# A mixture-of-experts and attention kernel on one core: slot table read first, no adds ahead of the first tile, tokens taken ahead of the gather

## What is computed

```
x = x + 0.5 * ffn(layernorm(x))
x = x + attn(layernorm(x))
x = x + 0.5 * ffn(layernorm(x))

ffn:  logits = x @ Wr;  two best of E = 8 experts per token, weights by softmax over the two
      pos = rank of the token within its expert;  kept = pos < cap  (cap = 2560)
      h = silu(xe @ W1[e]) * (xe @ W3[e])      (1024 wide)
      out[token] += weight * (h @ W2[e])
attn: KV = cumsum(K outer V);  Y = Q . KV per head (16 heads of 16);  a 16x16 map per head;  Y @ Wc.T
```

## Time and profile before

| | us |
|---|---|
| median of 3 runs | 3054.07 (3050.84 to 3055.57) |
| the profiled execution | 3048.99 |
| its span | 3047.3 |
| PE busy | 2854.6 (94%) |
| DVE, ACT, POOL busy | 1602.6, 1253.7, 1158.8 |
| mean granted clock of PE | 0.971 |

### The profile page before, as it was taken

The page is one execution under the profiler, slowest core; times in us unless marked ns, Lnnn a source line. Parts: engine busy times, 40 slices in busy tenths (PEclk is TensorE's granted clock), DMA queues, the critical chain, the costliest instruction groups (busy, mean ns, idle before and its releaser), DMA issues. The chain is left out here.

```text
span 3047.3 us, 54514 instructions
## 1 busy us (share of the span) xinstructions
PE 2854.6 (94%) x18727; PEld 2543.1 (83%) x18727; DVE 1602.6 (53%) x3791; ACT 1253.7 (41%) x2685; POOL 1158.8 (38%) x1560
## 2 busy tenths in 40 slices
PE   5379999999999999979999994999999999999997
PEld 3368898989899988868888884898998998898986
DVE  8843544454454545347778775345545454445443
ACT  5233434344444434334444442344434343444433
POOL 3654444444443434310111123443434443444432
PEclk9689999999999999989999996999999999999999
DMA  7542323232323312220111013323323232323221
GB/s 251 177 119 39 80 36 77 42 77 42 77 44 75 84 30 41 36 54 29 58 56 59 30 44 95 85 40 76 77 43 77 42 81 32 80 42 77 41 36 26
DMA packets 156550, 198.51 MB, mean 65 GB/s; under 512 B 15696, under 2 KB 128464, under 8 KB 156368
## 3 DMA queue, kind: packets, MB, share of 16 engines
q0 software_dynamic: 64128, 88.42, 17.6%
q1 hardware_dynamic: 81952, 97.30, 9.8%
q10 hardware_dynamic: 10288, 10.38, 1.0%
HBM read 124.32 MB, written 80.11 MB: 67 GB/s over the span
## 5 line engine op out<-in xcount | busy, mean ns | idle before, releaser
L1259 DVE TENSOR_TENSOR e_h_lo<-e_hid,e_h_hi 128x384 fp32r<-128x384 f32 (+1 forms) x640 | 383.7, 600 | 399.2 <-ACT e_h_hi L1219 399.2
L1256 DVE TENSOR_TENSOR e_hid<-e_ps,e_gate 128x384 f32<-128x384 f32 (+1 forms) x640 | 382.0, 597 | 308.4 <-ACT e_gate L1215 308.3
L1219 ACT ACTIVATE e_h_hi<-e_hid 128x384 fp32r<-128x384 f32 (+1 forms) x640 | 356.7, 557 | 444.1 <-DVE e_hid L1256 443.8
L1215 ACT ACTIVATE e_gate<-e_ps 128x384 f32<-128x384 f32 (+1 forms) x640 | 333.5, 521 | 330.7 <-PE e_ps L101 330.5
L99 PE MATMUL e_ps<-e_xT_hi,c_wa 128*128 128x384 f32 (+1 forms) x1280 | 454.5, 355 | 9.0 <-DVE e_yrow L1269 6.0
L99 PE MATMUL e_ps<-e_xT_hi,e_wb 128*128 128x384 f32 (+1 forms) x1280 | 460.3, 360 | 0.0
L100 PE MATMUL e_ps<-e_xT_lo,e_wb 128*128 128x384 f32 (+1 forms) x1280 | 455.1, 356 | 0.0
L101 PE MATMUL e_ps<-e_xT_hi,e_wb 128*128 128x384 f32 (+1 forms) x1280 | 455.0, 355 | 0.0
L101 PE MATMUL e_ps<-e_xT_hi,c_wa 128*128 128x384 f32 (+1 forms) x1280 | 449.7, 351 | 0.0
L100 PE MATMUL e_ps<-e_xT_lo,c_wa 128*128 128x384 f32 (+1 forms) x1280 | 449.7, 351 | 0.0
L433 POOL DMA_INDIRECT c_xrow<-normed_rows,e_token x320 | 347.8, 1087 | 156.6 <-issue 91.3
(11 more groups left out here) (297 smaller groups left out, 5189.5 us busy)
## 6 DMA issues: line engine op xcount, KB each, us to landing
c_raw<-w SPq DMA_DIRECT2D x204, 256.0 KB, 5.5
normed_rows<-r_xn SPq DMA_DIRECT2D x8, 1056.0 KB, 7.2
normed_rows<-mi_xn SPq DMA_DIRECT2D x8, 1056.0 KB, 4.7
x<-x ACTq DMA_DIRECT2D x8, 1024.0 KB, 12.3
out<-mi_x SPq DMA_DIRECT2D x8, 1024.0 KB, 5.3
r_xin<-x SPq DMA_DIRECT2D x7, 1024.0 KB, 11.0
c_raw<-x SPq DMA_DIRECT2D x7, 1024.0 KB, 8.1
c_xrow<-normed_rows,e_token POOLq DMA_INDIRECT x320
```

Of the source, the lines that this page charges most:

```text
L1215: act.activation(gate[:, f % 2, 0:n], ps1[f % 2][:, 0:n], ACT.Silu).then_inc(gated, 1)
L1219: act.activation(h[0][:, f, 0:n], hid[:, f % 2, 0:n], ACT.Copy).then_inc(h_high, 1)
L1256: dve.tensor_tensor(hid[:, f % 2, 0:n], ps3[f % 2][:, 0:n], gate[:, f % 2, 0:n], ALU.mult).then_inc(hid_ready, 1)
L1259: dve.tensor_tensor(h[1][:, f, 0:n], hid[:, f % 2, 0:n], h[0][:, f, 0:n].bitcast(F32), ALU.subtract).then_inc(h_ready, 1)
```

## The change

It has five parts.

1. `tiles` is split: `read_counts` keeps the one operation that reads PE's bank, where `tiles` stood; the other operations follow `read_table`, in the route phase behind the six `low_w` too, which themselves now follow `read_table`.
2. The first turn of an expert phase takes three blocks in place of four, waits for three gathers, and `high_x` and `low_x` behind it are 384 columns wide.
3. The single add of zeros and tile 0's four are gone; tile 1's four stay.
4. `meta(g + 1)` is done within tile g, behind its adds and ahead of its gather. `meta(0)` is done once ahead of the first tile, and the first expert is written out ahead of the loop over the other seven.
5. The loads of groups 1 and 2 of the middle phase's input are issued at the start of the middle phase.

```diff
+    def read_counts(self, dve):
+        dve.wait_ge(self.count_made, 1)
+        dve.tensor_scalar(self.lg[:, 0, :], self.rank_bank[:, self.RANK_AT:self.RANK_AT + E], float(CAP), float(P - 1),
+                          ALU.min, ALU.add).then_inc(self.count_read, 1)
...
     def tiles(self, dve, table):
...
-        dve.wait_ge(self.count_made, 1)
-        dve.tensor_scalar(units, self.rank_bank[:, self.RANK_AT:self.RANK_AT + E], float(CAP), float(P - 1), ALU.min,
-                          ALU.add).then_inc(self.count_read, 1)
...
     def load_x1(self, sp, x1, x1_g):
         for i in range(MG // 2):
             sp.dma_start(x1[:, 0, 2 * i:2 * i + 2], x1_g[0][:, 2 * i:2 * i + 2]).then_inc(self.x_first[i], 16)
-        for g in (1, 2):
-            sp.dma_start(x1[:, g], x1_g[g]).then_inc(self.x_loaded[g], 16)
...
-                r.tiles(dve, tiles_out)
+                r.read_counts(dve)
+                dve.wait_ge(r.tabled, T // P // QUAD)
+                r.read_table(dve, r.table_bank[:, 0:SCOLS], slot_token)
                 for q in range(LOW_BY_POOL, PIECES):
                     low_w(q)
-                dve.wait_ge(r.tabled, T // P // QUAD)
-                r.read_table(dve, r.table_bank[:, 0:SCOLS], slot_token)
+                r.tiles(dve, tiles_out)
...
-                def meta(g):
-
-                    pool.wait_ge(y_added, WORDS * g + 16)
+                def meta(g, adds):
+
+                    if adds:
+                        pool.wait_ge(y_added, WORDS * g - WORDS)
                     wait_alone(pool, held, g + 1, k.passed)
...
-                def tile(e, subs, at, behind, g):
-                    meta(g)
+                def tile(e, subs, at, behind, g, adds=True):
                     hold(e, subs, at, g)
-                    wait_alone(pool, y_kept, g + 1, k.passed)
-                    add(BIG)
+                    if adds:
+                        wait_alone(pool, y_kept, g + 1, k.passed)
+                        add(BIG)
+                    meta(g + 1, adds)
                     gather(behind, g)
...
-                wait_alone(pool, held, 1, k.passed)
-                add(1)
-                with pool.Fori(0, E) as e:
+                meta(0, False)
+                expert(0, adds=False)
+                with pool.Fori(1, E) as e:
                     expert(e)
 
                 n = total(pool)
-                meta(n)
                 wait_alone(pool, y_kept, n + 1, k.passed)
                 add(BIG)
-                pool.wait_ge(y_added, WORDS * n + WORDS + 16)
+                pool.wait_ge(y_added, WORDS * n)
...
-                def turn(n_loaded):
+                def turn(n_loaded, subs=BIG):
                     pe.wait_ge(x_loaded, n_loaded)
                     for half in range(KD):
-                        for sub in range(BIG):
+                        for sub in range(subs):
...
-                turn(WORDS)
+                turn(16 * SMALL, SMALL)
...
-                high_x(KD + 1)
+                high_x(KD + 1, SMALL * P)
...
-                low_x(1)
+                low_x(1, SMALL * P)
...
+                load(1)
+                load(2)
                 for g in range(MGS):
                     sp.wait_ge(x2_ready, MG * (g + 1))
...
                     if n == NCH + COUNT:
-                        r.tiles(dve, tiles_out)
+                        r.read_counts(dve)
...
                 dve.drain()
                 r.read_table(dve, tab[:], slot_token)
+                r.tiles(dve, tiles_out)
```

More of the change, by code:

```diff
@@ L1082, in hold, with expert @@
                     pool.tensor_copy(next_token[:, 0:subs], slot_token[:, bass.ds(at, subs)]).then_inc(next_held, 1)
-                def tile(e, subs, at, behind, g):
-                    meta(g)
+                def tile(e, subs, at, behind, g, adds=True):
                     hold(e, subs, at, g)
-                    wait_alone(pool, y_kept, g + 1, k.passed)
-                    add(BIG)
+                    if adds:
+                        wait_alone(pool, y_kept, g + 1, k.passed)
+                        add(BIG)
+                    meta(g + 1, adds)
                     gather(behind, g)
-                def expert(e):
+                def expert(e, adds=True):
                     f, big, small = counts(pool, e)
                     at = e * UPE
-                    tile(e, SMALL, at, pool.snap(at + SMALL), f)
+                    tile(e, SMALL, at, at + SMALL if isinstance(e, int) else pool.snap(at + SMALL), f, adds)
                     with pool.Fori(0, big) as t:
@@ L1133, in _ @@
                 add(SMALL)
-                wait_alone(pool, y_added, WORDS * n + WORDS + 16 * SMALL + 16, k.passed)
+                wait_alone(pool, y_added, WORDS * n + 16 * SMALL, k.passed)
                 pool.nop().then_inc(all_added, 1)
@@ L1201, in high_w, with high_x @@
                     act.activation(piece(slots[1 - s][:, 0], q), piece(raw, q), ACT.Copy).then_inc(w_high, 1)
-                def high_x(n):
+                def high_x(n, width=WIDE):
                     for half in range(KD):
                         act.wait_ge(x_turned, n + half)
-                        act.activation(xT[0][:, half, :], psx[:, half, :], ACT.Copy).then_inc(x_high, 1)
+                        act.activation(xT[0][:, half, 0:width], psx[:, half, 0:width], ACT.Copy).then_inc(x_high, 1)
                 def tile(e, s, subs, first, at, g):
@@ L1243, in low_w, with low_x @@
                                       ALU.subtract).then_inc(w_low, 1)
-                def low_x(n):
+                def low_x(n, width=WIDE):
                     for half in range(KD):
                         dve.wait_ge(x_high, n + half)
-                        ins = dve.tensor_tensor(xT[1][:, half, :], psx[:, half, :], xT[0][:, half, :].bitcast(F32),
-                                                ALU.subtract)
+                        ins = dve.tensor_tensor(xT[1][:, half, 0:width], psx[:, half, 0:width],
+                                                xT[0][:, half, 0:width].bitcast(F32), ALU.subtract)
                     ins.then_inc(x_ready, 1)
```

## The result

| | before | after |
|---|---|---|
| median of 4 runs, us | 3054.82 (3050.84 to 3055.69) | 3019.20 (3017.54 to 3019.95) |
| profiled execution, its span | 3048.99, 3047.3 | 3019.95, 3018.2 |

The ratio is 0.9885, with an interval of 0.9868 to 0.9902; 3022.9 was forecast. In three later series the kernel before had medians of 3052.68, 3052.90 and 3054.98, and the changed kernel, run once more, 3020.71 (3018.94 to 3021.25).

The account below looks back on a forecast made before the run. TensorE bounds the expert phases without gaps; gains lie in stalls at their starts and between blocks. 5.6 + 3.4 + 1.0 + 9.2 + 6.0 + 6.0 = 31.2 us off 3054.07 gave 3022.9 us, range 3015 to 3034.

Parts of the forecast that it names:

- turn stalls: Expert phases' starts: PE's waits for tile 1's gather, 1.97 and 7.24 us, would go, 9.2 us.
- read-out stalls: Expert phases' starts: tile 1's second banks waiting for tile 0's results to be read out, 3.58 + 2.44 = 6.0 us, would go.
- the clock: Behind three of the four stalls PE's granted clock was 0.66 to 0.84; full speed would return 6.0 us, ends 4 and 6.
- The route phase's end: Slot table read ahead of counts and low parts: route block ends 5.6 us sooner, ends 3.6 and 5.9.
- so SP is late next: Route phase's end: SP, done at 155.5, rather than POOL's drain (152.4 to 155.4) would end the block; 155.7 taken.
- The counts of the middle phase: Middle phase's end: counts leave the chain ahead of the picks and the gather, gaining 3.4 us.
- the narrow turn: Tile 0 of each expert phase: first transpose to first matmul, 3.44 us, shortens by 0.5 us a phase, 1.0 us.
- Part 4 at nothing: Every tile: waiting for the adds' landing ahead of the gather, 3.0 to 7.1 us, hides under 9.3 us cover; cost 0.
- A: Rival at the route phase's end: VectorE's subtracts and counts hold the gather, 3026.6 us; chance 0.12.
- C: Rival: blocks end as before, POOL's drain not set by the gather's landing, 9.0 us fail, 3031.9 us; chance 0.04.
- D: Rival in all tiles: POOL becomes the bound through the landing wait ahead of the gather, 3060 us and over; chance 0.03.
- B: Rival in tile 1: the four adds of zeros that stay keep the read-out stall, 3030.6 us; chance 0.08.

Follow-up runs that it names:

- Experiment ten: Changed kernel with expert 1's weights loaded at the start of expert phase 1's block, not at the route phase's end: 3016.29 us.
- experiment nine: Changed kernel plus six 128x512 VectorE subtracts with unused output behind the middle phase's table read, beside a gather without weight loads: 3020.69 us.
- experiment one: Changed kernel with the slot table reads again behind counts and low parts, and the middle phase's counts ahead of the last picks: 3028.03 us.
- experiment six: Changed kernel with two more indirect adds in each full tile, to rows nobody reads: 3019.57 us.
- experiment three: Changed kernel with the five adds of zeros back, tokens still taken ahead of the gather: 3051.02 us.

## Why the prediction was right

The mechanism was the one forecast: POOL's adds of zeros held the second gather and the tokens, and without them all four stalls go. The turn stalls and read-out stalls came out at the forecast sizes to 0.1 us, and the clock behind them at 5.3 for 6.0. Undoing parts 3 and 4 together gave 25 us for the 21.2 of these three terms (its stalls are 16.5 us, the kernel before's 15.2, and its clock took 8.3).

*The route phase's end* was forecast as 5.6 and was 4.6; over the nine profiles with the early gather it is 3.9 to 4.9. The slots came at 143.99 (144.3), and SyncE was done at 154.9 (155.5). The failed step is "so SP is late next": POOL's drain stayed last. I had bracketed it with 11.1 us after the slots beside the weight loads, and it took 12.1. Experiment ten shows that the loads are 3.6 to 4.2 us of that. Of the 1.0 us by which it overshot the bracket, the gather beside the subtracts is 0.3 (4.61 us for 4.33). The rest may be that an earlier gather meets more of the loads: the profiles with the late gather have the two smallest values, but no run separates this.

*The counts of the middle phase* gave 3.6 for 3.4, *the narrow turn* 1.4 for 1.0 in the two timelines, and 0.67 us a phase again in its own experiment's trace. The rule that the chain is half fixed was cautious; most of a quarter came off (2.77 for 3.44 us).

*Part 4 at nothing* held, but for a reason that I gave only in part. The cover of 9.3 us a tile is there from tile 1 on. In tile 0 there is none, and the order is free there only because part 3 took out the adds whose landing it would wait for. The forecast should have named that dependence; together the two were priced rightly.

*Part 5 at nothing* held: with the loads back the time is the same. The missed items are the POOL drains of the expert phases, 1.3 us gained, the start of the middle phase, 2.8 us lost between two profiles, and 0.65 us in the route phase ahead of the table, which the change doesn't touch. Together they are -0.85 us: that the total came so close is partly that they cancel. The first goes and comes with part 3 (5.54 and 5.54 us with the five adds, 4.88 without, 5.05 with two more adds a tile); what sets it stays open.

*The median.* The profiled execution of before lay 5.8 us below its final median; that of after lay 0.75 above. I had carried an offset of 5.1 us over from one profile to the other. That put the forecast 5.1 + 0.75 = 5.8 us too high; that 31.2 as a difference of profiles was 2.1 too much took it back to 3.7 us above 3019.2. The two errors partly cancel, and that is luck.

*The rivals.* A fell with experiment nine, C with experiment one (8.8 us), D with experiment six, which found another 3.7 us of room a tile. B, that the adds that stay keep the read-out stall, fell with the profile: the tokens came at 182.82, 5.8 us before ACT needs them. The forecast was 188 on the old clock, which is 182.7 when the block before ends 5.3 us sooner. Its mechanism, a late landing, is real all the same: experiment three shows it with 6.13 us.

## What to carry to other kernels

When a ring or pipeline is filled with work that carries nothing, count what is queued behind it on its engine in the first rounds: five of nine adds of zeros cost some 25 us here, in a kernel whose steady state has no gap; the four that stayed cost TensorE no wait. Price a reordering in the first round apart from the others; the same order cost 6.5 us or nothing, depending on whether something had just been sent. A block here ends with its slowest drain, and twelve weight loads on another queue lengthened it by 3.6 to 4.2 us: what isn't needed soon is better issued on the far side of the barrier. Profile a kernel more than once before you read an item of 1 or 2 us from a difference of two profiles.

## What was not expected of the hardware

- POOL's drain behind four gathers took 8.7 to 10.4 us beside twelve weight loads (9.7 and 10.4 in two profiles of one program) and 6.1 to 6.2 without them.
- Six VectorE subtracts beside four gathers stretched these by 0.3 to 0.6 us in all (4.61 for 4.33, 4.79 for 4.23) and were not slowed themselves in the route phase (3.69 us in both).
- POOL's drain at an expert phase's end, behind adds that have all landed, took 4.88, 5.05 or 5.54 us, the same to 0.01 us in both phases of a program and in all programs with the same adds. What sets it stays open.
- Behind 14 and 12 transposes at 2.4 GHz, TensorE stood 3.6 and 3.8 us, made six transposes, stood 1.3 us, and began the next block's matmuls at 1.2 GHz.
- At the start of the middle phase the granted clock reached 0.89 to 0.91 between 4 and 8 us and in one of two profiles fell back to 0.53 for some 7 us more, with the same instructions and transfers.
